# Normed rows on ScalarE, their scale and sum on GpSimd, and a later place for the second norm's means, in a fused tokenizer, scan and experts kernel

## The chip, the cores and the metric

The kernel runs on one core of one Trainium2 chip. The metric is the device time of one launch in microseconds (us), as the median of several runs. A core has five engines that work side by side: TensorE (PE in the rows; its weight loads are PEld), VectorE (DVE), ScalarE (ACT), GpSimd (POOL) and SyncE (SP), which here only issues DMAs. Each takes its instructions in the order written for it, and stands still where one of them waits for a semaphore. [...]

## The reference

Images become tokens, a selective scan mixes them, and a mixture of experts follows. What the change touches is the layer norm before the scan, the layer norm after it, the residual sum, and the statistics of the third norm. Cut down:

```
h = concat(tokens(x), txt)                      # 4 x 384 rows of 192 channels
a = in_proj(layernorm(h))                       # first norm
u = silu(conv(a_x)); dt = softplus(u @ dt_w.T + dt_b)
s_t = exp(dt * A_n) * s_(t-1) + dt * B_n * u    # for each of 16 states n
y = sum_n(C_n * s_n) + D * u
r = (y * silu(a_z)) @ out_w.T + layernorm(h)
h = h + (r - mean(r)) / std(r) * ln_g + ln_b    # second norm, scale, shift
logits = layernorm(h) @ Wr.T                    # third norm; top 2 of 8 experts
h = h + experts(layernorm(h))
```

## The kernel before

The 1536 rows are held as 12 tiles of 128 rows, in NJ = 3 groups j of NB = 4 tiles; `h_tok[:, j, b, :]` is one tile with its 192 channels. A group is also a chunk of 128 time steps. The scan goes through 48 steps: `at` runs from 0 to 47, the chunk is n = at // 16 and the state is s = at % 16. Chunk 0 still has the first norm, projections and convolution of the last group mixed into it; chunks 1 and 2 have the output of the chunk before mixed in.

One step `at` is spread over all engines, and each engine's order is written out by hand:

- SP issues the broadcast of row C of the step (`broadcast_c`, three DMAs, as soon as the product three steps back is done), sometimes a row B (`broadcast_b`), and a part of the experts' weights (`load_expert`). At steps 30 and 46 it also waits for `xf_rdy` and sends a group's router rows to DRAM (`send_rows`).
- TensorE spreads row B over the partitions (`spread_b(at)`, L983 to L986, except for steps with at % 6 == 5), does the step's extra work or a filler (L1053), and then adds the product of two steps back into `sums` (`sum_states(at - 2)`, L1005 and L1007). So `spread_b(at)` stands behind `sum_states(at - 3)` in its queue.
- ScalarE saves the last state of the chunk (`save_carry`, L1443), brings the state carried over from the chunk before (`bring_carry(at + 1)`, L1455; it waits for `spread_b(at + 1)`), and makes exp(dt * A) (`decay_of(at + 2)`, L1437 and L1438). At step 24 (and 40) follow `deviation` (Sqrt, L1306) for the second norm, at 25 (41) for the third norm, and at 28 (44) `router_rows` (L1462), which makes the third norm's rows. Changing between Exp and Sqrt costs a table load.
- VectorE multiplies by row B (L1752, not in the steps with at % 6 == 5) and runs the scan over all six blocks of channels (L1760). In front of scan 24 `residual` takes means and variances of the output rows in PSUM (`means`, L1586 and L1591) and makes (r - mean) * ln_g (`normed_rows`, L1776). Behind scan 24 come the reciprocal (`inverse`, L1602), four small operations on the router's scores, `new_h` (L1807, h + that * rstd) with the third norm's means, and behind scan 26 `row_shift` (L1602, L1816). Steps 39 to 42 repeat it for group 1. After the last step group 2 is done in pieces.
- GpSimd multiplies the states by row C (L697, product `at`; waits for scan `at`), and for the steps with at % 6 == 5 also by row B (`pool_drive`, L686). At step 24 (40) it first waits for `h_new`, and at 26 (42) for `shift_rdy`, so that these products don't start earlier. `add_shift` (L661) adds ln_b to a group of h.

Two buffers hold the states, so scan `at` waits for product `at - 2` and for the carry of step `at - 2`. The rows of the first norm of the last group are made by VectorE behind scan 4 (`input_norm(2)`, L1606); TensorE's transposes, and GpSimd's product 4, wait for them (`xn_ready`).

```
elif s == 8:                       # GpSimd, before
    pool.wait_ge(h_new, n)
elif s == 10:
    pool.wait_ge(shift_rdy, n)
```

Of the kernel before, what the change touches and what calls it, by code (L numbers as in the profile page):

```python
# [19 lines left out]
ALU = mybir.AluOpType  # L20
# [3 lines left out]
P = 128  # L24
NB = 4
C = 192
CB = C - P
NJ = 3
# [115 lines left out]
def build(nc, d, out):  # L144
    with ExitStack() as ctx:
# [26 lines left out]
        shift = sb("shift", [P, NT])  # L172
        bo = sb("bo", [P, C])
# [227 lines left out]
        shift_rdy = sem("shift_rdy")  # L401
        top_step = sem("top_step")
# [123 lines left out]
        def _(sp):  # L526
# [77 lines left out]
            for at in range(RING, STEPS):  # L604
                if at == S - 3:
                    store_bc(2)
                broadcast_c(at)
                if at == S - 2:
                    sp.wait_ge(bc_stored, 16 * 8)
                if by_pool(at - RING) and at - RING + 6 < STEPS:  # L610
                    broadcast_b(at - RING + 6)
                if at > S and at % S == 14:
                    send_rows(at // S - 1)
                if at == S:
                    sp.wait_ge(xt_ready, 6)
                    sp.wait_ge(dtu_rdy, 3)
                if at == 2 * S + 7:
                    sp.wait_ge(summed, 2 * S + 1)
                    sp.dma_start(u_cm[:, 0:N_TAB // 2], d["cst"][:, N_CST:N_CST + N_TAB // 2]).then_inc(ld_tab, 16)
                if at >= S and at % 4 != 3 and loaded < len(loads):  # L620
                    load_expert(*loads[loaded], PIECES)
                    loaded += 1
            assert loaded == len(loads)
            sp.wait_ge(summed, STEPS)
            for e in range(E - LATE, E - 1):
                load_expert(e, 0, 1)
            send_rows(2)
# [15 lines left out]
        def _(pool):  # L643
# [19 lines left out]

            def inserted_work(n, s):

                if n == 0:
                    if s == 4:
                        pool.wait_ge(xn_ready, 3)
                    elif s == 7:
                        pool.wait_ge(conv_step, 8 * 3)  # L670
                    elif s == 11:
                        pool.wait_ge(split_step, 5 * 3)
                    elif s == 13:
                        pool.wait_ge(dtu_rdy, 3)
                elif s == 8:
                    pool.wait_ge(h_new, n)
                elif s == 10:
                    pool.wait_ge(shift_rdy, n)
# [10 lines left out]
            for at in range(STEPS - 1):  # L689
                if at in (1, 5, S + 2):  # L690
                    add_shift(at // 4 if at < S else 2)
                pool.wait_ge(scanned, at + 1)
# [517 lines left out]
        def _(act):  # L1210
# [206 lines left out]

            act.wait_ge(a_exp, 2)
# [51 lines left out]
            for at in range(STEPS):  # L1470
# [9 lines left out]
                if n == 0:  # L1480
# [4 lines left out]
                    elif s == 4:  # L1485
                        deviation(2)
                    elif s == 5:
# [24 lines left out]
                else:  # L1512
                    if s == 8:
                        deviation(1 + 2 * n)
                    elif s == 9:
                        deviation(2 + 2 * n)
                    elif s == 12:
                        router_rows(n - 1)
# [37 lines left out]
        def _(dve):  # L1556
# [95 lines left out]

            def input_norm(n):
                j = JS[n]
                inverse()
                for b in range(NB):
# [122 lines left out]
            def residual(j):  # L1779
                dve.wait_ge(attn_ps, j + 1)  # L1780
                means([attn_rows(j, b)[:, 0:C] for b in range(NB)])
                for b in range(NB):
                    ins = normed_rows(j, b)
                ins.then_inc(rr_rdy, 1)
                dve.wait_ge(rr_rdy, j + 1)
# [18 lines left out]
            def new_h(j):  # L1804
# [4 lines left out]
                ins.then_inc(h_new, 1)  # L1809
                dve.wait_ge(h_new, j + 1)  # L1810
# [28 lines left out]
            for at in range(STEPS):  # L1839
# [14 lines left out]
                else:  # L1854
# [4 lines left out]
                    elif s == 8:  # L1859
                        if n == 1:  # L1860
                            dve.wait_ge(hb_rdy, NJ)
# [3 lines left out]
                        new_h(n - 1)  # L1865
# [3 lines left out]
                    elif s == 10:  # L1869
# [61 lines left out]
            dve.wait_ge(rr_rdy, NJ + 1)  # L1931
            new_h(2)
# [171 lines left out]
```

## Time and profile before

| | us |
|---|---|
| median of 3 runs | 431.66 |
| lowest, highest | 430.48, 434.25 |
| span of the profiled execution | 431.6 |

| scan step (L1760) | starts at | | scan step | starts at |
|---|---|---|---|---|
| 4 | 90.52 | | 30 | 183.36 |
| 7 | 99.08 | | 33 | 191.79 |
| 16 | 137.79 | | 35 | 197.02 |
| 23 | 155.69 | | 36 | 202.01 |
| 24 | 161.39 | | 39 | 210.18 |
| 25 | 169.23 | | 40 | 215.88 |
| 26 | 172.85 | | 41 | 221.69 |
| 28 | 178.48 | | 46 | 236.28 |
| 29 | 180.34 | | 47 | 238.02 |

The profile's times count from the first instruction. The span agrees with the median to 0.1 us, so sums made inside the profiled execution can be read against the median directly. The scan is the stretch from 78 to 240 us; before it lie the first two norms and projections, behind it the routing (to 269) and the experts (to the end). The rows show for each instruction its start, its length, its engine, line and tiles, and in brackets how long the engine stood idle in front of it and who released it.

### The profile page before, as it was taken

To read this page: it belongs to the slowest core of one execution; us is meant where nothing else is said; L and a number is where in the kernel's file an instruction comes from. 1 tells how busy PE (TensorE), PEld (TensorE's weight loads), DVE (VectorE), ACT (ScalarE), POOL (GpSimd) and SP (SyncE) were. 2 spreads that over 40 slices of the span, in tenths; PEclk is the share of its full clock that TensorE was granted. 3 is DMA by queue.
4 is the path that set the end of the run, shared out by engine and by line. 5 is a ranking of instruction groups with operands and counts; after the bars stand their busy time and mean duration, and the time that the engine had idled before them with its cause. 6 is when DMAs were issued, how large, how long until landed. Compare 5 with 4: busy or idle time off the path is not lost.

```text
span 431.6 us, 6906 instructions
## 1 busy us (share of the span) xinstructions
PE 379.8 (88%) x2285; PEld 286.8 (66%) x2285; DVE 276.2 (64%) x511; ACT 200.5 (46%) x516; POOL 224.0 (52%) x166
## 2 busy tenths in 40 slices
PE   5799989979996995779968898999999999999970
PEld 4465756646564662445634486799999999999970
DVE  4605456999899998997999596643444534434400
ACT  1347447674853546734547023144444354354440
POOL 6877730564636772756637200345565554655531
PEclk9969899999989996998979997799999999999995
DMA  6401103446574875497857544433333233232224
GB/s 168 78 6 11 7 3 70 122 120 137 116 147 122 232 243 165 158 270 210 294 167 189 150 209 74 113 83 59 49 46 61 43 49 56 44 52 48 39 28 118
DMA packets 37351, 46.98 MB, mean 109 GB/s; under 512 B 9485, under 2 KB 25950, under 8 KB 36750
## 3 DMA queue, kind: packets, MB, share of 16 engines
q1 hardware_dynamic: 29998, 38.94, 32.1%
q0 software_dynamic: 7328, 7.74, 12.2%
q8 instruction: 12, 0.20, 0.2%
q14 instruction: 13, 0.11, 0.1%
HBM read 40.65 MB, written 7.19 MB: 111 GB/s over the span
## 4 chain that ended last, share of the span: by engine, by line
PE 60%; DVE 17%; ACT 6%; DMA 5%; POOL 5%; issue 3%; SPq 1%; POOLq 0%; DVEq 0%; ACTq 0%
PE ps L1190 15%; PE ps L1171 10%; PE ps L1179 6%; DVE w_all L1760 5%; PE ps L1005 4%; DMA w_all<-bc_dram 3%; PE ps L1053 3%; PE ps L934 3%; POOL w_all L647 3%; POOL w_all L697 2%; DVE ps L1752 2%; PE ps L1007 2%; PE ps L1161 2%; DVE stats L1586 1%; DVE h_tok L1807 1%
## 5 line engine op out<-in xcount | busy, mean ns | idle before, releaser
L697 POOL TENSOR_TENSOR w_all<-w_all 128x768 f32<-128x768 f32 x47 | 78.9, 1682 | 82.4 <-DVE w_all L1760 36.6
L722 POOL DMA_INDIRECT sum_dram<-u_cm,tok_row x31 | 50.9, 1641 | 60.5 <-ACT u_cm L1551 53.8
L1005 PE MATMUL ps<-w_all,cst 128*128 128x512 f32 x96 | 55.4, 661 | 22.9 <-POOL w_all L697 22.3
L1760 DVE TENSOR_TENSOR_SCAN w_all<-decay,ps 128x780 f32<-128x780 f32 x40 | 71.1, 1779 | 2.0 <-POOL w_all L697 0.7
L706 POOL DMA_INDIRECT dt_cm<-x_dram,tok_in x31 | 30.8, 993 | 41.0 <-DVE texi L1989 29.0
L647 POOL DMA_INDIRECT w_all<-in_pix,gidx x42 | 44.1, 1051 | 14.9 <-issue 12.5
L1536 ACT ACTIVATE u_cm<-ps,x_cm 128x128 f32<-128x128 f32 x96 | 26.5, 376 | 39.8 <-PE ps L1179 39.8
L934 PE MATMUL ps<-cst 128*128 128x256 f32 x132 | 36.5, 433 | 5.5 <-DMA cst<-in_cst 4.9
L1005 PEld LDWEIGHTS ps<-w_all,cst 128*128 128x128 f32 x96 | 16.5, 198 | 35.4 <-POOL w_all L697 30.4
L1752 DVE TENSOR_TENSOR ps<-dtu_cm,ps 128x768 f32<-128x768 f32 x40 | 38.0, 949 | 2.7 <-ACT ps L1455 2.5
L1536 ACT ACTIVATE z_cm<-ps,y_cm 128x128 f32<-128x128 f32 x90 | 24.8, 375 | 27.5 <-PE ps L1179 27.5
L934 PEld LDWEIGHTS ps<-cst 128*128 128x128 f32 x132 | 28.0, 219 | 12.6 <-DMA cst<-in_cst 4.9
L2001 DVE COPY x_cm<-w_all 128x1154 f32 x16 | 12.2, 762 | 37.1 <-PE ps L1190 37.1
L1007 PEld LDWEIGHTS ps<-w_all,cst 128*128 128x128 f32 x96 | 19.2, 200 | 24.9 <-issue 24.9
L1190 PE MATMUL ps<-x_cm,u_cm 128*128 128x192 f32 x192 | 35.5, 333 | 0.0
L1053 PE MATMUL ps<-cst 128*128 128x256 f32 x122 | 33.6, 401 | 0.0
L1190 PE MATMUL ps<-y_cm,z_cm 128*128 128x192 f32 x180 | 33.4, 334 | 0.0
L2001 DVE COPY y_cm<-w_all 128x1154 f32 x15 | 11.4, 762 | 33.0 <-PE ps L1190 33.0
L1437 ACT ACTIVATE decay<-dt_cm,a_neg 128x512 f32<-128x512 f32 x40 | 28.4, 711 | 8.2 <-DVE dt_cm L1709 8.1
L1190 PEld LDWEIGHTS ps<-x_cm,u_cm 128*128 128x128 f32 x192 | 31.0, 189 | 1.8
L1190 PEld LDWEIGHTS ps<-y_cm,z_cm 128*128 128x128 f32 x180 | 29.0, 189 | 1.8
L1007 PE MATMUL ps<-w_all,cst 128*128 128x256 f32 x96 | 30.1, 396 | 0.0
(268 smaller groups left out, 706.8 us busy)
## 6 DMA issues: line engine op xcount, KB each, us to landing
w_all<-bc_dram SPq DMA_DIRECT2D x48, 256.0 KB, 3.6
w_all<-bc_dram SPq DMA_DIRECT2D x96, 64.0 KB, 3.8
w_all<-in_w_all SPq DMA_DIRECT2D x20, 289.0 KB, 4.5
w_all<-in_w_all SPq DMA_DIRECT2D x3, 1156.0 KB, 8.9
b_wide_sb<-bc_dram SPq DMA_DIRECT2D x8, 256.0 KB, 3.9
x_dram<-x_cm SPq DMA_DIRECT2D x3, 384.0 KB, 4.6
sum_dram<-h_tok SPq DMA_DIRECT2D x3, 384.0 KB, 4.3
out<-sum_dram SPq DMA_DIRECT2D x4, 288.0 KB, 3.7
```

What stands on the lines that cost most here:

```text
L647: pool.indirect_dma_start(dst, None, d[table], bass.IndirectOffsetOnAxis(ap=gidx[:, col:col + 1].bitcast(U32), axis=0)).then_inc(signal, 16)
L697: nc.gpsimd.tensor_tensor(segments(hcs[at % 2]), inner(states[at % 2]), segments(c_sb[at % RING]), ALU.mult).then_inc(hc_rdy, 1)
L722: pool.indirect_dma_start(sum_dram, bass.IndirectOffsetOnAxis(ap=tok_row[:, i:i + 1].bitcast(U32), axis=0), y_out[:, i % 2, :], None, comp ...
L934: nc.tensor.matmul(ps[:, bank, 0:256], ident, cst[:, 0:256], start=True, stop=True)
L1005: nc.tensor.matmul(sums[:, 0:4 * P], ident, hcs[at % 2][:, 0:4 * P], start=False, stop=at % S == S - 1, skip_group_check=True)
L1007: nc.tensor.matmul(sums[:, 4 * P:6 * P], ident, hcs[at % 2][:, 4 * P:6 * P], start=False, stop=at % S == S - 1, skip_group_check=True).the ...
L1053: nc.tensor.matmul(ps[:, bank, 256:512], ident, cst[:, 0:256], start=False, stop=True, skip_group_check=True)
L1171: nc.tensor.matmul(ps[:, 2 + 2 * p + f // 3, P * (f % 3):P * (f % 3) + P], w[:, W_UA + P * f:W_UA + P * f + P], xe[:, p, 0:P], start=(f % ...
L1190: mm = nc.tensor.matmul(ps[:, 6 + p, 0:C], hid[p][:, P * f:P * f + P], w_now[p][:, W_DN + C * f:W_DN + C * f + C], start=(f == 0), stop=(f ...
L1536: ins = nc.scalar.activation(hid[p][:, P * f:P * f + P], ps[:, 2 + 2 * p + f // 3, P * (f % 3):P * (f % 3) + P], ACT.Gelu, bias=w_now[p][: ...
L1752: v.tensor_tensor(inner(wide(p)), chunk(dtu3, n), inner(wide(p)), ALU.mult).then_inc(driven, 1)
L1760: v.tensor_tensor_scan(states[p], fade, drive, 0.0, ALU.mult, ALU.add).then_inc(scanned, 1)
```

## The change

For groups 0 and 1 (chunks 1 and 2) the second norm's rows move from VectorE to ScalarE, as Identity with scale rstd and bias -mean * rstd (`fall`, one small VectorE operation, `row_fall`). GpSimd multiplies them by ln_g in two operations of 128x384 at s == 9 (`scale_rows`) and adds them to h in two more at s == 11 (`add_rows`), which now signals `h_new`. VectorE takes the third norm's means at s == 12 and the row shift at s == 13; ScalarE takes that norm's deviation at s == 13 and the router rows at s == 14. GpSimd's two waits at s == 8 and s == 10 go. The first norm of the last group is made by ScalarE too. SP sends group 0's rows at step 34 instead of 30, and group 1's behind the last step instead of at 46. Group 2's norm after the scan stays on VectorE.

```diff
@@ sync
-                if at > S and at % S == 14:
-                    send_rows(at // S - 1)
+                if at == 2 * S + 2:
+                    send_rows(0)
...
                 load_expert(e, 0, 1)
+            send_rows(1)
             send_rows(2)
@@ gpsimd
+            def scale_rows(j):
+                pool.wait_ge(rows_normed, j + 1)
+                for two in (ip_a, ip_b):
+                    rows = two[:, :].rearrange("p (b c) -> p b c", b=2)
+                    ins = nc.gpsimd.tensor_tensor(rows, rows, ln_gb[:, 0:1, :].to_broadcast([P, 2, C]), ALU.mult)
+                ins.then_inc(scaled, 1)
+
+            def add_rows(j):
+                pool.wait_ge(scaled, j + 1)
+                for h, two in ((0, ip_a), (1, ip_b)):
+                    ins = nc.gpsimd.tensor_tensor(h_tok[:, j, 2 * h:2 * h + 2, :], h_tok[:, j, 2 * h:2 * h + 2, :],
+                                                  two[:, :].rearrange("p (b c) -> p b c", b=2), ALU.add)
+                ins.then_inc(h_new, 1)
...
-                elif s == 8:
-                    pool.wait_ge(h_new, n)
-                elif s == 10:
-                    pool.wait_ge(shift_rdy, n)
...
+                if at >= S and at % S == 9:
+                    scale_rows(at // S - 1)
+                elif at >= S and at % S == 11:
+                    pool.wait_ge(hb_rdy, NJ)
+                    add_rows(at // S - 1)
                 pool.wait_ge(scanned, at + 1)
@@ scalar
+            def last_input_rows():
+                j = JS[2]
+                act.wait_ge(fall_rdy, 1)
+                for b in range(NB):
+                    t = NB * j + b
+                    ins = nc.scalar.activation(xn[:, j, b, 0:C], h_tok[:, j, b, :], ACT.Identity, bias=fall[:, 0, t:t + 1],
+                                               scale=rstd[:, 0, t:t + 1])
+                ins.then_inc(xn_ready, 1)
+
+            def normed_rows(j):
+                act.wait_ge(fall_rdy, j + 2)
+                if j:
+                    act.wait_ge(h_new, j)
+                for b in range(NB):
+                    t = NB * j + b
+                    ins = nc.scalar.activation(rr(b), attn_rows(j, b)[:, 0:C], ACT.Identity, bias=fall[:, 1, t:t + 1],
+                                               scale=rstd[:, 1, t:t + 1])
+                ins.then_inc(rows_normed, 1)
...
                     elif s == 4:
                         deviation(2)
+                        last_input_rows()
...
                     if s == 8:
                         deviation(1 + 2 * n)
-                    elif s == 9:
+                        normed_rows(n - 1)
+                    elif s == 13:
                         deviation(2 + 2 * n)
-                    elif s == 12:
+                    elif s == 14:
                         router_rows(n - 1)
@@ vector
+            def row_fall(norm, j):
...
+                v.scalar_tensor_tensor(fall[:, norm, t], mv[:, norm, t, 0], -1.0, rstd[:, norm, t], ALU.mult, ALU.mult)\
+                    .then_inc(fall_rdy, 1)
...
                 inverse()
+                if n == 2:
+                    row_fall(0, j)
+                    return
...
                 means([attn_rows(j, b)[:, 0:C] for b in range(NB)])
-                for b in range(NB):
-                    ins = normed_rows(j, b)
-                ins.then_inc(rr_rdy, 1)
-                dve.wait_ge(rr_rdy, j + 1)
...
                     elif s == 8:
-                        if n == 1:
-                            dve.wait_ge(hb_rdy, NJ)
                         inverse()
                         unscaled_scores(n - 1)
                         router_scores(n - 1)
-                        new_h(n - 1)
+                        row_fall(1, n - 1)
                     elif s == 9:
                         largest(n - 1)
                         its_experts(n - 1)
-                    elif s == 10:
+                    elif s == 12:
+                        h_means(n - 1)
+                    elif s == 13:
                         row_shift(n - 1)
```

`h_means` is the second half of `new_h` (wait for `h_new`, then the means of the group of h). `new_h` itself is left for group 2 alone, under the name `last_h`, and waits there for `hb_rdy`.

## Rows read from the trace of the kernel before

**Rows 1.** The cores: span and mean granted clock
```profile
core 0: 431.6 us, clock 0.941
```

**Rows 2.** Stretches from:to, length, busy us (count) by engine, clock, DMA share, GB/s
```profile
158.00:184.00 26.00, 18.23 (x72) 10.47 (x71) 24.09 (x54) 17.03 (x40) 13.39 (x8) 0.87 0.56 175
```

**Rows 3.** Who waited for whom, 130 to 245 us: total us, times, longest us
```profile
POOL w_all L697 <- DVE h_tok L1807: 11.9, 2, 7.2
```

**Rows 4.** Timeline, VectorE, chunk 0 (start, length, operation, [idle before])
```profile
92.40 1.25 DVE L1606 TENSOR_SCALAR xn<-h_tok,mv,rstd 128x192 f32<-128x192 f32 x4
99.08 1.78 DVE L1760 TENSOR_TENSOR_SCAN w_all<-decay,ps 128x780 f32<-128x780 f32 x1 [0.21 <-POOL w_all L697]
```

**Rows 5.** Timeline, GpSimd: product 4
```profile
93.78 1.68 POOL L697 TENSOR_TENSOR w_all<-w_all 128x768 f32<-128x768 f32 x1 [3.24 <-DVE xn L1606]
```

**Rows 6.** Timeline, VectorE, step 24 to scan 26
```profile
158.97 0.74 DVE L1776 SCALAR_TENSOR_TENSOR ip_a<-ps,mv,ln_gb 128x192 f32<-128x192 f32 x2
...
164.09 0.18 DVE L1602 RECIPROCAL rstd<-std 128x4 f32<-128x4 f32 x1 [0.93 <-ACT std L1306]
...
165.21 0.75 DVE L1807 SCALAR_TENSOR_TENSOR h_tok<-ip_a,rstd,h_tok 128x192 f32<-128x192 f32 x2
...
166.65 1.14 DVE L1586 BATCH_NORM_STATS2 stats<-h_tok 128x6 f32<-128x192 f32 x4
...
169.23 1.78 DVE L1760 TENSOR_TENSOR_SCAN w_all<-decay,ps 128x780 f32<-128x780 f32 x1
...
172.85 1.78 DVE L1760 TENSOR_TENSOR_SCAN w_all<-decay,ps 128x780 f32<-128x780 f32 x1
...
174.73 0.16 DVE L1816 SCALAR_TENSOR_TENSOR shift<-mv,rstd 128x4 f32<-128x4 f32 x1
```

**Rows 7.** Timeline, ScalarE, steps 24 to 30
```profile
163.90 0.20 ACT L1443 ACTIVATE carry<-w_all 128x6 f32<-128x6 f32 x1
...
172.14 0.18 ACT L1455 ACTIVATE ps<-carry 128x6 f32<-128x6 f32 x1 [0.88 <-PE ps L986]
172.34 1.28 ACT L1437 ACT_TABLE_LOAD   x1
173.63 0.72 ACT L1437 ACTIVATE decay<-dt_cm,a_neg 128x512 f32<-128x512 f32 x1
174.26 0.49 ACT L1438 ACTIVATE decay<-dt_cm,a_neg 128x256 f32<-128x256 f32 x1
...
179.91 1.85 ACT L1462 ACTIVATE x_cm<-h_tok,shift,rstd 128x192 f32<-128x192 f32 x4
...
182.15 0.18 ACT L1455 ACTIVATE ps<-carry 128x6 f32<-128x6 f32 x1 [0.29 <-PE ps L986]
```

**Rows 8.** Timeline, TensorE: sums of product 24, of 27, and of 40
```profile
168.47 2.07 PE L1005 MATMUL ps<-w_all,cst 128*128 128x512 f32 x2 [4.31 <-POOL w_all L697]
...
180.17 1.12 PE L1005 MATMUL ps<-w_all,cst 128*128 128x512 f32 x2 [1.42 <-POOL w_all L697]
...
221.94 2.08 PE L1005 MATMUL ps<-w_all,cst 128*128 128x512 f32 x2 [3.28 <-POOL w_all L697]
```

**Rows 9.** The page's groups by line, and by form: GpSimd (busy us, mean ns, idle before)
```profile
L697 POOL TENSOR_TENSOR w_all<-w_all 128x768 f32<-128x768 f32 x47 | 78.9, 1682 | 82.4 <-DVE w_all L1760 36.6 <-DVE h_tok L1807 11.9 <-DVE dtu_cm L1711 8.0
L686 POOL TENSOR_TENSOR decay<-dtu_cm,b_wide_sb 128x768 f32<-128x768 f32 x8 | 14.5, 1817 | 0.0
L661 POOL TENSOR_TENSOR h_tok<-h_tok,ln_gb 128x768 f32<-128x768 f32 x3 | 5.5, 1817 | 0.0
L2094 POOL MEMSET const-uint8-127<- 128x1 uint8 x1 | 0.1, 119 | 0.0
```

**Rows 10.** Timeline, VectorE, chunk 2: what it waited for
```profile
201.01 0.96 DVE L1752 TENSOR_TENSOR ps<-dtu_cm,ps 128x768 f32<-128x768 f32 x1 [2.24 <-ACT ps L1455]
...
240.90 0.96 DVE L1836 TENSOR_TENSOR w_all<-w_all 128x768 f32<-128x768 f32 x1 [1.09 <-DMA w_all<-bc_dram]
243.50 0.96 DVE L1764 TENSOR_TENSOR y_cm<-ps,z_cm 128x768 f32<-128x768 f32 x1 [1.65 <-PE ps L1007]
```

More of the change, by code:

```diff
@@ L172, in build @@
         shift = sb("shift", [P, NT])
+        fall = sb("fall", [P, 2, NT])
         bo = sb("bo", [P, C])
@@ L401, in build @@
         shift_rdy = sem("shift_rdy")
+        fall_rdy = sem("fall_rdy")
+        rows_normed = sem("rows_normed")
+        scaled = sem("scaled")
         top_step = sem("top_step")
@@ L1651, in input_means @@
                 means([h_tok[:, JS[n], b, :] for b in range(NB)])
+            falls = 0
+            def row_fall(norm, j):
+                nonlocal falls
+                falls += 1
+                t = slice(NB * j, NB * j + NB)
+                v.scalar_tensor_tensor(fall[:, norm, t], mv[:, norm, t, 0], -1.0, rstd[:, norm, t], ALU.mult, ALU.mult)\
+                    .then_inc(fall_rdy, 1)
             def input_norm(n):
@@ L1802, in router_scores, with last_h @@
                 scored(v.tensor_tensor(logit[:, t, :], logit[:, t, :], p1[:, t, :], ALU.add))
-            def new_h(j):
+            def last_h():
+                j = NJ - 1
                 for b in range(NB):
@@ L1809, in new_h, with h_means @@
                 ins.then_inc(h_new, 1)
+                h_means(j)
+            def h_means(j):
                 dve.wait_ge(h_new, j + 1)
@@ L1930, in _ @@
             ins.then_inc(rr_rdy, 1)
-            dve.wait_ge(rr_rdy, NJ + 1)
-            new_h(2)
+            dve.wait_ge(rr_rdy, 2)
+            dve.wait_ge(hb_rdy, NJ)
+            last_h()
             rt(v.tensor_tensor(gtmp[:, 1, :], top_v[:, :, 1], top_v[:, :, 0], ALU.subtract))
```

## The prediction, made before the changed kernel ran

> **What bounds the kernel now.** I read the cores first: the span is 431.6 us [rows 1], equal to the median. The change lies in the scan, so I went by stretches: while group 0's output is mixed in, VectorE is busy 24.1 of 26 us [rows 2]. Then the timelines. The scan goes at VectorE's pace, some 2.7 us a step (0.96 and 1.78, less their overlap [rows 10]), except where a wait shows: 0.93 for the standard deviation behind scan 24 [rows 6]; 2.24 at step 36 and 1.09 for the last row C [rows 10]. GpSimd waits much longer for h_new, 11.9 us in two places [rows 3], but its product is wanted only two scans later. So taking work from VectorE is worth its time where VectorE has the last word, and nothing where ScalarE, TensorE or GpSimd have it. The question is which of them is late next.
>
> **What is removed.** VectorE loses four L1776 and four L1807 in each of two groups. A pair takes 0.74 [rows 6], four of a kind 1.4, so 2.8 a group; and L1606 with 1.25 [rows 4]. It gains three `row_fall` like L1816 with 0.16 [rows 6]. Net 2 x 2.8 + 1.25 - 0.5 = 6.4 us less. The third norm's means are moved, not removed: 1.14 [rows 6] and 0.38 for the four aggregates, 1.5.
>
> **Prices of what is added.** ScalarE: four Identity rows of 192 with scale and bias take 1.85 [rows 7]. GpSimd: no 128x384 operation is in the trace. The 128x768 ones take 1.68 to 1.82, the smallest memset 0.12 [rows 9], so little of the price is fixed and a half costs 0.85 to 0.95; two make 1.85. The other bound is that a half costs as much as a whole, 1.8 each.
>
> [...]
>
> Whether Identity wants a table of its own behind Sqrt no row shows; a load is 1.28 [rows 7], and the nearest row is a Copy straight behind the Sqrt, without one [rows 7]. I take nothing, and keep 1.28 for the range.
>
> [...]
>
> **Chunk 0, +0.85.** VectorE ended the input rows at 92.40 + 1.25 = 93.65 [rows 4], and product 4 followed at once [rows 5]. Now: `row_fall` to 92.6, ScalarE's four to 94.5. VectorE is free 1.1 earlier and scan 5 moves up, but product 4 starts 0.85 later, behind it GpSimd's `add_shift` and product 5, and scan 7 already waited 0.21 for that product [rows 4]. TensorE's projection also follows the same rows. Both paths move by 0.85, and nothing up to chunk 1 takes it back. Below I use the old clock, without this shift.
>
> **Chunk 1, to step 30.**
> - Without L1776 scan 24 starts 1.4 earlier. But the standard deviation comes at 164.0 as before: ScalarE reaches it behind its carry and decay, which hang on TensorE's queue. The wait of 0.93 becomes 2.3. Gain nothing.
> - Behind the reciprocal the scores end at 165.21 [rows 6]. L1807 and the means go from there (1.4 + 1.5, to 168.2), `row_fall` comes. Scan 25 starts at 166.35 instead of 169.23, 2.9 ahead; scan 26 at 166.35 + 3.62 (the old distance [rows 6]) = 169.97, to 171.75.
> - ScalarE's rows take 165.4 to 167.3, GpSimd's scale to 169.2, product 25 to 170.9. Scan 27 wants it at 172.65 or later: hidden.
> - GpSimd then has product 26 (from 171.85), the row-B product for step 29, `add_rows`, product 27: 1.65 + 1.77 + 1.85 + 1.65 = 6.9, to 178.75. That is the new late one. The means of step 28 start at 177.1 (`h_new`) and end at 178.7, and scan 29 waits for product 27: 178.8 to 180.6, 1.45 ahead.
> - TensorE adds product 27 and only then spreads row B of step 30; ScalarE's carry for 30 waits for that, then comes decay 31, and *then* the moved `deviation`. This is the worst place of the change. Old distance from the sum's start to ScalarE's carry: 180.17 to 182.15 = 2.0 at full clock, 168.47 to 172.14 = 3.7 where TensorE had idled 4.31 [rows 7, 8]. TensorE idles here from about 175.5 to 178.8, 3.3 us. Idles of 3.28 and 4.31 were followed by a sum at half pace (2.08 and 2.07), one of 1.42 was not [rows 8]; I take the slow one. The carry ends at 180.9 or 182.6.
> - Decay 0.72 + 0.49 less overlap 1.1, load 1.28 [rows 7], and 0.3 for the Sqrt (the four-element operations beside it take 0.2): 2.7. The deviation is there at 183.6 or 185.3, where VectorE has been idle since 180.6. With `row_shift` 0.35 and the row-B product 0.95 scan 30 starts at 185.0 or 186.7, before 183.36: 1.6 or 3.3 behind, after having been 3.1 ahead at scan 28.
>
> **Chunk 1, to step 36.** ScalarE's load, decay, router rows (4.2 together) and carry end about 1 us before scan 31 does: hidden, barely. `send_rows(0)` no longer holds up SP at step 30, so the rows C of steps 31 and 32 come in time, TensorE isn't starved at 189 to 192, and most of the 2.24 at step 36 [rows 10] and another 0.4 in front of step 33 go. At step 34 the same 384 KB lie before row C of step 35, which has over 2 us to spare. Step 36 is 0.35 ahead (full clock) or 1.2 behind (slow): I take 1.05 behind.
>
> **Chunk 2, -2.2.** Here VectorE waited for no deviation, so the first 1.4 count too: 1.4 + 2.9 = 4.3 ahead at scan 41 and 4.4 at 44. Step 44 gives back 1.5 for the means: 2.8 ahead. There is no row-B product of GpSimd between product 42 and `add_rows(1)`, so product 43 is in time and the deviation comes at 232.2, just before scan 45 ends; at the slow clock 1.1 late. Decay 47 stands behind a table load, about 0.4. The 1.09 for the last row C goes, since SP has no `send_rows` in front of it, but the sums of 46 and 47 must still follow each other on TensorE. `chunk_output(2)` was at 243.50 [rows 10]; it comes at 240.7 (2.8 ahead) or 241.75 (1.75 ahead). Middle 2.2. Behind it nothing changes; `send_rows(1)` has 20 us to land.
>
> **Sum.** 431.6 + 0.85 + 1.05 - 2.2 = 431.3 us. The saving of 6.4 and the two waits are nearly all spent on ScalarE's and GpSimd's later answers.
>
> **Rivals.**
> 1. *The same path, TensorE at full clock.* 431.6 + 0.85 - 0.35 - 2.8 = 429.3. For it: busy work is pulled forward, the old idle of 4.31 goes. Against: the new idle of 3.3.
> 2. *VectorE has the last word throughout* (faster). All 6.4 count, and the 2.24: 431.6 - 8.6 = 423.0. For it: it is busy 93% of this stretch [rows 2]. Against: the order on ScalarE at step 29, and the two waits already there. It needs the deviation of step 29 ready by 181.
> 3. *GpSimd's halves cost as much as wholes* (slower). Scale and sum take 3.6 each: product 25 ends at 172.7 and pushes product 26 by 0.85, the sum pushes product 27 by another 1.8, so 2.65 in chunk 1, and some 3 in chunk 2 by the same queue. 431.3 + 5.7 = 437.0. Against: the memset's 0.12 [rows 9]. It passes 1% from about 1.6 us for a half.
> 4. *Identity loads a table*: 1.28 at each of three places on the path, 431.3 + 3.8 = 435.1, within 1%.
>
> **How the numbers follow.** One per cent, 4.3 us, is about what a measurement of this kernel can tell from no change. Forecast 0.46, rival 1 0.22, rival 2 0.14, rival 3 0.10, rival 4 0.04; 0.04 for other losses over 1%. So faster 0.14, same 0.72, slower 0.14. The time is that of the likeliest, 431.3. The range leaves out rivals 2 and 3 with most of their chance, and takes in 1 and 4 with 1.3 us below 429.3 for links that I have sized by one row: 428.0 to 435.1.
>
> **What would show it.** Scan 7 at about 99.9. Scan 25 2.9 nearer to scan 24's old place. The four ScalarE rows 1.85, GpSimd's halves 0.85 to 0.95. VectorE idle about 3 to 4.5 us in front of the reciprocal between scans 29 and 30, released by ScalarE; TensorE idle over 3 us before the sum of product 27, and the granted clock at 0.5 behind it. No DMA wait before the last product, and none of 2 us before step 36. If the reciprocal in front of step 30 waits for nothing, rival 2 is right; if the halves take over 1.6, rival 3.

## The result, and the profile after

The changed kernel takes 434.69 us (median of 20 runs, 430.16 to 439.77); the kernel before takes 432.45 us in the same comparison (20 runs, 428.08 to 440.05). The ratio is 1.0059, with a 95% interval of 1.0034 to 1.0084: about 2.5 us slower, 1.5 to 3.6. I had forecast 431.3 us and no change. The time lies in my range, the sign doesn't agree.

The page of the kernel after (busy us, share of the span, instructions). Before, VectorE was busy for 276.2 us, ScalarE for 200.5 and GpSimd for 224.0:

```profile
PE 377.9 (88%) x2285; PEld 285.8 (67%) x2285; DVE 272.5 (63%) x494; ACT 205.7 (48%) x528; POOL 229.9 (53%) x174
```

```profile
core 0: 429.8 us, clock 0.948
```

The clock is the one granted to TensorE on the mean, as a share of full speed.

VectorE did get 3.7 us less work (I had reckoned with 6.4; 1.5 of the difference is the row shift of 1.67 us shown below, which counts as busy time), and the span is even 1.8 us shorter than that of [rows 1]. Neither is the result. The spans differ in their long tail and in the time up to scan 4, which the change doesn't touch: scan 4 starts at 85.4 to 93.5 us from one execution to another, of either order. So I compare the stretches between starts of scans. "End" is the last `chunk_output(2)` (L1764, now L1822). Each number is worked out from the timeline of VectorE:

| scans | before | before, 2nd | after | after, 2nd |
|---|---|---|---|---|
| 4 to 16 | 47.27 | 47.28 | 49.41 | 47.72 |
| 16 to 28 | 40.69 | 40.67 | 37.83 | 37.85 |
| 28 to 30 | 4.88 | 4.89 | 9.22 | 9.22 |
| 30 to 36 | 18.65 | 16.48 | 16.47 | 16.46 |
| 36 to 40 | 13.87 | 13.87 | 12.44 | 12.45 |
| 40 to 44 | 15.06 | 15.06 | 13.11 | 11.92 |
| 44 to 47 | 7.08 | 7.09 | 10.41 | 10.40 |
| 47 to end | 5.48 | 5.06 | 4.77 | 4.78 |
| sum | 152.98 | 150.40 | 153.66 | 150.80 |

Most stretches repeat to 0.02 us. The others belong to an execution: the 2.2 us that I read in the kernel before (30 to 36) isn't in its second execution, and the kernel after has two of that kind (4 to 16, 40 to 44).

What is given back between scans 28 and 30: the timelines of VectorE and ScalarE of the kernel after (start, length, operation, idle before).

```profile
176.14 1.78 DVE L1818 TENSOR_TENSOR_SCAN w_all<-ps,decay 128x780 f32<-128x780 f32 x1
180.81 0.18 DVE L1647 RECIPROCAL rstd<-std 128x4 f32<-128x4 f32 x1 [2.89 <-ACT std L1328]
```

```profile
177.95 0.18 ACT L1498 ACTIVATE ps<-carry 128x6 f32<-128x6 f32 x1 [3.05 <-PE ps L1008]
178.06 0.71 ACT L1480 ACTIVATE decay<-dt_cm,a_neg 128x512 f32<-128x512 f32 x1
178.68 0.49 ACT L1481 ACTIVATE decay<-dt_cm,a_neg 128x256 f32<-128x256 f32 x1
179.18 1.28 ACT L1328 ACT_TABLE_LOAD   x1
180.48 0.30 ACT L1328 ACTIVATE std<-mv,cst 128x4 f32<-128x4 f32 x1
```

VectorE stands 2.89 us for a Sqrt of 0.30, behind a carry, a decay and a table load. What is given back in chunk 2, VectorE and GpSimd:

```profile
219.81 0.96 DVE L1810 TENSOR_TENSOR ps<-dtu_cm,ps 128x768 f32<-128x768 f32 x1 [0.45 <-ACT ps L1498]
...
223.12 0.96 DVE L1810 TENSOR_TENSOR ps<-dtu_cm,ps 128x768 f32<-128x768 f32 x1 [0.53 <-ACT ps L1498]
...
230.25 1.67 DVE L1874 SCALAR_TENSOR_TENSOR shift<-mv,rstd 128x4 f32<-128x4 f32 x1
```

```profile
215.20 1.68 POOL L719 TENSOR_TENSOR w_all<-w_all 128x768 f32<-128x768 f32 x1 [2.56 <-DMA w_all<-bc_dram]
...
230.22 1.68 POOL L719 TENSOR_TENSOR w_all<-w_all 128x768 f32<-128x768 f32 x1 [0.81 <-DVE w_all L1818]
```

The row shift over 128x4 took 0.16 us in [rows 6] and takes 1.67 here. It starts 0.03 us behind product 45 of GpSimd and ends with it. The profile shows no idle time for it: the loss is inside an instruction's length.

### The profile page after: what moved, and what is told of

Same layout as the page of the kernel before. It is cut to its first block, busy times and chain, and to the rows that moved or that the text cites. A ratio compares the mean times of both kernels' runs of the same rounds, so it can differ in the third digit from the quotient of the medians.

```text
span 429.8 us, 6909 instructions
## 1 busy us (share of the span) xinstructions
PE 377.9 (88%) x2285; PEld 285.8 (67%) x2285; DVE 272.5 (63%) x494; ACT 205.7 (48%) x528; POOL 229.9 (53%) x174
## 3 DMA queue, kind: packets, MB, share of 16 engines
q0 software_dynamic: 7328, 7.74, 12.3%
## 4 chain that ended last, share of the span: by engine, by line
PE 59%; DVE 15%; ACT 7%; POOL 7%; DMA 4%; issue 4%; SPq 1%; POOLq 0%; DVEq 0%; ACTq 0%
PE ps L1212 15%; PE ps L1193 10%; PE ps L1201 6%; DVE w_all L1818 5%; PE ps L1027 4%; POOL w_all L719 3%; DVE ps L1810 2%; POOL w_all L652 2%; PE ps L956 2%; DMA w_all<-bc_dram 2%; PE ps L1075 2%; PE ps L1029 2%; PE ps L1183 2%; ACT decay L1480 1%; PE ps L890 1%
## 5 line engine op out<-in xcount | busy, mean ns | idle before, releaser
L744 POOL DMA_INDIRECT sum_dram<-u_cm,tok_row x31 | 49.7, 1602 | 63.2 <-ACT u_cm L1596 60.6
L956 PE MATMUL ps<-cst 128*128 128x256 f32 x132 | 35.8, 426 | 5.5 <-DMA cst<-in_cst 4.9
L1075 PE MATMUL ps<-cst 128*128 128x256 f32 x122 | 33.0, 395 | 0.0
```

Source lines behind the costliest of these rows:

```text
L744: pool.indirect_dma_start(sum_dram, bass.IndirectOffsetOnAxis(ap=tok_row[:, i:i + 1].bitcast(U32), axis=0), y_out[:, i % 2, :], None, comp ...
L956: nc.tensor.matmul(ps[:, bank, 0:256], ident, cst[:, 0:256], start=True, stop=True)
L1075: nc.tensor.matmul(ps[:, bank, 256:512], ident, cst[:, 0:256], start=False, stop=True, skip_group_check=True)
```

## The experiments

Sums below are scan 4 to the end, as in the table. A ratio is against the kernel before on the same chip.

**The kernel before, and the kernel after, once more** (nothing is edited; one execution each).

> The kernel before once more, for a second profile. Theory 5: the 2.2 us stall in front of step 36, which I counted as removed, belongs to some executions only (e2, which keeps the transfer at step 30, doesn't have it): scan 30 to 36 takes 16.5 us here. Rival: the stall belongs to the kernel and takes 18.6 again; then e2's 16.5 comes from its shift of 0.8 us.

> A further execution of the changed kernel itself. The stretches that the instructions' order sets should repeat within 0.1 us: 28 to 30 9.2, 44 to 47 10.4, 24 to 28 15.7, 36 to 40 12.4. Where TensorE's clock chooses, it may differ: 4 to 7 10.2 if the loss of chunk 0 belongs to the kernel, 9.4 if it belongs to the execution shown first.

They are the columns "2nd" above. The stall of step 36 is in some executions of the kernel before only. Of the loss in chunk 0, 1.7 of 2.1 us, and 1.2 us of chunk 2 belong to the first execution of the kernel after. The two least disturbed executions differ by 0.4 us only (150.80 against 150.40).

TensorE, product 31's sum and the fillers behind it, in the kernel before, first the execution of [rows 10]:

```profile
191.65 1.13 PE L1005 MATMUL ps<-w_all,cst 128*128 128x512 f32 x2 [2.37 <-POOL w_all L697]
...
193.74 2.77 PE L1053 MATMUL ps<-cst 128*128 128x256 f32 x6
```

and its second execution:

```profile
189.69 1.13 PE L1005 MATMUL ps<-w_all,cst 128*128 128x512 f32 x2 [1.89 <-POOL w_all L697]
...
191.42 1.46 PE L1053 MATMUL ps<-cst 128*128 128x256 f32 x6
```

GpSimd waits 3.01 and 2.54 us for row C there. In the first TensorE idled 2.37 us and the six fillers took 2.77 us instead of 1.46. Windows over this place (length, busy time of PE, PEld, DVE, ACT, POOL, then granted clock, DMA share, GB/s), the first from the kernel before, the second from its second execution:

```profile
190.00:196.20 6.20, 4.55 (x14) 3.37 (x15) 5.71 (x6) 2.31 (x8) 6.20 (x4) 0.74 0.94 288
```

```profile
188.00:192.70 4.70, 3.01 (x14) 2.16 (x15) 4.67 (x5) 1.71 (x6) 4.70 (x3) 1.00 0.91 297
```

**The last input rows back on VectorE, and on ScalarE alone.**

```diff
@@ the changed kernel, rows on VectorE again
-                if n == 2:
-                    row_fall(0, j)
-                    return
...
-                        last_input_rows()
@@ the kernel before, rows on ScalarE
+                        last_input_rows()
...
+                if n == 2:
+                    t = slice(NB * j, NB * j + NB)
+                    v.scalar_tensor_tensor(fall[:, 0, t], mv[:, 0, t, 0], -1.0, rstd[:, 0, t], ALU.mult, ALU.mult)\
+                        .then_inc(fall_rdy, 1)
+                    return
```

> The changed kernel, with the last group's input rows back on VectorE (its L1606), all else kept. [...] Theory 2 (the wait of 2.9 us for the deviation behind scan 29) and theory 3 (the moved row transfers make the end later): it stays at 1.005, with at most 0.9 us gained.

> The kernel before, with only the last group's input rows moved to ScalarE. [...] Theories 2 and 3: slower by the 0.85 us that I forecast, 1.002, the clock unchanged.

Back on VectorE: ratio 1.0014 (0.9959 to 1.0070), chunk 0 as before, 47.29. On ScalarE alone: ratio 1.0008 (0.9961 to 1.0056), 0.8 us more between scans 4 and 7 and 0.35 less between 8 and 16, so 47.73. Moving these rows costs 0.4 us where TensorE keeps its clock. It did in six of the seven executions with the rows on ScalarE: from 2.5 to 8 us behind the start of ScalarE's rows the granted clock was 1.00 in the six and 0.69 in the seventh. So the whole loss of 0.6% doesn't lie in chunk 0: ScalarE's rows alone cost 0.4 us and not the 2.1 of the first execution of the kernel after, and the profile with the rows back on VectorE has a sum of 153.97, no less than the 153.66 of the kernel after. In the seventh execution, the kernel after as shown first, the clock fell. Windows from scan 5 on, kernel after and its second execution:

```profile
90.30:100.00 9.70, 9.14 (x47) 5.27 (x48) 6.14 (x7) 5.95 (x15) 6.14 (x4) 0.82 0.45 115
```

```profile
95.40:105.00 9.60, 9.03 (x56) 5.70 (x56) 7.53 (x10) 6.76 (x16) 6.15 (x4) 1.00 0.45 117
```

TensorE had idled 1.24 and 1.66 us just before in both.

**Fillers in front of the transposes of these rows.**

```diff
                     elif s == 6:
+                        filler(4)
                         norm_transposes(2)
```

> The changed kernel with four fillers of TensorE in front of the transposes of the last input rows (step 6), which TensorE ran behind an idle of 1.66 us in all executions with the rows on ScalarE, while its clock fell behind them in one of four. The theory that this idle decides expects it cut to about 1 us or less and, from scan 4 to 7, 9.4 us as at full clock. The rival, that the clock at this place hangs on what came earlier, allows 10.2 here too. One execution can refute the first and only lean towards it.

9.36 from scan 4 to 7, with a granted clock of 1.00 from 94.80 to 100.30 (sum 151.27, one run of 433.65). The unedited kernel has 9.36 too in its second execution, so this run tells nothing about the idle. It is inconclusive.

**The second deviation in front of the carry and the decay.**

```diff
@@ scalar, step s == 13
+                    deviation(2 + 2 * n)
                     bring_carry(at + 1)
                     decay_of(at + 2)
...
-                    elif s == 13:
-                        deviation(2 + 2 * n)
```

> The changed kernel, with ScalarE's third-norm deviation of step 29 (and 45) put in front of the carry and decay of that step instead of behind them. Theory 2: VectorE's wait of 2.9 us in front of the reciprocal goes, the Exp table's load then lies in front of decay 31, hidden beside scans 29 and 30; 2.5 us faster than the changed kernel, 1.000 of before. [...]

The stretch from 28 to 30 takes 7.74 us instead of 9.22, a gain of 1.5 us where I expected 2.5, and the ratio is 1.0076 (1.0037 to 1.0115), no better. The reciprocal no longer waits, but the row shift behind it runs beside product 29. VectorE and GpSimd of this run:

```profile
184.03 0.15 DVE L1647 RECIPROCAL rstd<-std 128x4 f32<-128x4 f32 x1
184.21 1.67 DVE L1874 SCALAR_TENSOR_TENSOR shift<-mv,rstd 128x4 f32<-128x4 f32 x1
```

```profile
184.19 1.67 POOL L719 TENSOR_TENSOR w_all<-w_all 128x768 f32<-128x768 f32 x1 [0.45 <-DVE w_all L1818]
```

**Only SP's transfers moved** (twice).

```diff
@@ the kernel before, sync
-                if at > S and at % S == 14:
-                    send_rows(at // S - 1)
+                if at == 2 * S + 2:
+                    send_rows(0)
...
+            send_rows(1)
             send_rows(2)
```

> The kernel before, with only SP's two row transfers moved (group 0 to step 34, group 1 behind the last step). By my sum: the stall of 2.2 us at step 36, 0.4 in front of scan 33 and part of the 1.1 for the last row C go: 2 to 3.5 us faster, 0.992 to 0.995. Theory 3: the transfer behind the experts' weights or the one at step 34 costs as much at the end or later: 1.000 to 1.005.

> The kernel before with only the moved transfers of the router rows, once more: it tells whether the moved transfers are worth something by themselves. If the stall of 2.24 us at step 36 in the profile of before is in some of its executions only, and the wait for the last row C (1.1 us) in all, the transfers are worth about 0.4 (47 to the last output, 5.06 to 4.74) plus a share of 2.2: a ratio of 0.995 to 0.999. If the stall were in all executions, 0.993 or below. If the transfers do nothing, 1.000. From scan 30 to 36 16.5 us.

Ratios 0.9941 (0.9894 to 0.9987) and 0.9970 (0.9935 to 1.0004); sums 150.07 and 150.05, without the stall, and 4.74 us from scan 47 to the end. This is the part of the change that is worth something by itself, 0.3 to 0.6 per cent; the second interval just includes no change. With the transfer at step 30 the stretch from 30 to 36 took 18.65, 16.48, 16.46, 16.87 and 18.75 us in five executions; without it never more than 16.86 in fourteen.

**GpSimd's two waits taken from the kernel before, and one given to the changed kernel.**

```diff
@@ the kernel before, gpsimd
-                elif s == 8:
-                    pool.wait_ge(h_new, n)
-                elif s == 10:
-                    pool.wait_ge(shift_rdy, n)
@@ the changed kernel, gpsimd
+                elif s == 13:
+                    pool.wait_ge(shift_rdy, n)
```

> The kernel before, without GpSimd's two waits (for h_new at steps 24 and 40, for shift_rdy at 26 and 42), nothing else changed; its products read and write none of those tensors. Theory 4 (a VectorE operation with two SBUF inputs stands still while a GpSimd product runs, as the 1.67 us row shift of the changed kernel at step 45 and of e3 at step 29 suggest): row_shift in steps 26 and 42 takes 1.67 instead of 0.16, some L1807 of group 1 take up to 1 us more; from scan 24 to 28 it is 1.5 us longer (18.6), from 40 to 44 1.5 to 2.3 longer (16.6 to 17.3), in all 3 to 4 us slower, 1.007 to 1.009. Rival: the 1.67 is a wait of another kind (a late semaphore), then both stretches keep 17.1 and 15.1 and the time is that of before or less.

> The changed kernel, with a wait of GpSimd for shift_rdy put in front of product 29 and 45. Theory 4: the row shift of step 45 takes 0.16 again, scan 44 to 47 takes 8.9 us instead of 10.4, and the kernel is 1.5 us faster than the changed one, 1.002 of before. Rival: no change in that stretch.

Without the waits the kernel before loses 2.0 us from 24 to 28 and 2.8 us from 40 to 44; its ratio is 1.0102 (1.0039 to 1.0166). Its row shift takes 1.67:

```profile
177.37 1.67 DVE L1812 SCALAR_TENSOR_TENSOR shift<-mv,rstd 128x4 f32<-128x4 f32 x1
```

```profile
177.34 1.68 POOL L693 TENSOR_TENSOR w_all<-w_all 128x768 f32<-128x768 f32 x1 [1.93 <-DVE w_all L1756]
```

That is 1.5 us in each chunk. The rest is the same clash at other operations. In chunk 1 the first operation of the scores starts 1.06 us behind product 24, takes 0.66 us instead of 0.19 and ends with the product (0.5 us). In chunk 2 the first two L1803 (L1807 in the kernel before) start 0.18 us behind product 40 and take 2.05 us instead of 0.74 (1.3 us):

```profile
166.47 0.66 DVE L1789 TENSOR_TENSOR logit<-mv,g_sum 128x32 f32<-128x32 f32 x1
...
220.91 2.05 DVE L1803 SCALAR_TENSOR_TENSOR h_tok<-ip_a,rstd,h_tok 128x192 f32<-128x192 f32 x2
```

```profile
165.41 1.68 POOL L693 TENSOR_TENSOR w_all<-w_all 128x768 f32<-128x768 f32 x1 [3.65 <-DMA w_all<-bc_dram]
...
220.73 1.68 POOL L693 TENSOR_TENSOR w_all<-w_all 128x768 f32<-128x768 f32 x1 [2.81 <-DMA w_all<-bc_dram]
```

VectorE's multiplication by row B, with one input in PSUM, keeps its 0.94 us although it starts in the middle of product 25:

```profile
174.51 0.94 DVE L1748 TENSOR_TENSOR ps<-dtu_cm,ps 128x768 f32<-128x768 f32 x1
```

```profile
173.73 1.68 POOL L693 TENSOR_TENSOR w_all<-w_all 128x768 f32<-128x768 f32 x1 [6.64 <-DVE w_all L1756]
```

With one wait the changed kernel gains what was expected, 8.90 instead of 10.41 from 44 to 47, and its ratio is 0.9970 (0.9920 to 1.0020). VectorE and GpSimd of that run, the same place as the 1.67 of the kernel after:

```profile
232.83 0.16 DVE L1876 SCALAR_TENSOR_TENSOR shift<-mv,rstd 128x4 f32<-128x4 f32 x1
```

```profile
233.13 1.68 POOL L721 TENSOR_TENSOR w_all<-w_all 128x768 f32<-128x768 f32 x1 [1.13 <-DVE shift L1876]
```

Product 45 starts 0.4 us behind its scan instead of 0.1, and nobody misses it. The sum of product 45 on TensorE, in the second execution of the kernel after and in this run:

```profile
238.66 1.12 PE L1027 MATMUL ps<-w_all,cst 128*128 128x512 f32 x2 [2.90 <-POOL w_all L719]
```

```profile
237.50 1.12 PE L1029 MATMUL ps<-w_all,cst 128*128 128x512 f32 x2 [1.07 <-POOL w_all L721]
```

The clash also opens an idle of 2.90 us on TensorE. In six executions without the wait (the idle was 2.90 us in five and 2.29 in one) a sum behind the idle ran slowly in three (1.92 to 2.08 us instead of 1.02 to 1.12), and scan 47 to the end took 6.2 to 6.5 us instead of 4.8; in the six executions with the wait it was 4.8 or 4.9 each time.

**All three mends** (input rows on VectorE, deviation first, GpSimd's wait), twice.

> The changed kernel with the three mends together: last group's input rows on VectorE, deviation in front of carry and decay, GpSimd's wait for shift_rdy at steps 29 and 45. If the parts add: chunk 0 as before (8.6 and 7.3 us), scan 28 to 30 6.2 us instead of 9.2, scan 44 to 47 8.9 instead of 10.4. From scan 16 to 47 2.9 us less than before without its stall at step 36; with the moved transfers 0.987 to 0.991 of before. If another wait takes their place: 0.995 or more.

> The kernel with all three mends once more, for an interval: the changed kernel, with the last input rows back on VectorE, the second deviation of a chunk in front of the carry and the decay, and GpSimd waiting for the row shift. Its profile had 4.0 us less than an undisturbed execution of the kernel before from scan 4 to the chunk's last output (146.4 against 150.4). The theory that VectorE's work does count once the late answers and the clash with GpSimd are gone expects a ratio of 0.991 (4.0 of 432), 0.985 to 0.996. The rival, that the low median of the earlier runs came from where TensorE's clock happened to stand in them, expects 0.998 to 1.002. From scan 28 to 30 6.3 us and from 44 to 47 8.9 us in both.

The first comparison gives 428.19 us (6 runs, before 433.26; no ratio), the second 427.81 with a ratio of 0.9869 (0.9832 to 0.9906): 5.7 us faster than the kernel before. From 28 to 30 it is 6.28 and 6.29 us, from 44 to 47 8.91. The sums are 146.40 and 149.01; they differ in the stretch from 40 to 44, with 11.98 and 14.46. With the moved transfers alone the sums were 150.07 and 150.05.

**The transfer of 1 MB behind the row.** In the second profile of the three mends product 40 waited 4.28 us for row C, and SP issues 1 MB (`u_cm<-in_cst`, for the routing) at step 39, in front of that row.

```profile
211.58 1.69 POOL L721 TENSOR_TENSOR w_all<-w_all 128x768 f32<-128x768 f32 x1 [4.28 <-DMA w_all<-bc_dram]
```

```diff
-                if at == 2 * S + 7:
+                if at == 2 * S + 11:
```

> The changed kernel with SP's transfer of 1 MB (the routing table, into u_cm) issued at step 43 instead of step 39, where it lies in front of row C of step 40. If the row's lateness is what varied, scan 40 to 44 takes 11.9 us (four steps of 2.67 and 1.26 of small operations) and product 40 waits 0.5 us at most; from 44 to 47 10.4 as before. In time 0.9 us less than the changed kernel's mean, a ratio of 1.000 to 1.005 against the kernel before. If something else makes it vary, 40 to 44 stays between 12 and 14. What could spoil it: the 1 MB now lies in front of rows C of 46 and 47 and a wait shows before the last product.

> The three mends (last input rows on VectorE, second deviation in front of carry and decay, GpSimd waiting for the row shift) and the transfer of 1 MB at step 43. Its last execution took 14.46 us from scan 40 to 44, with product 40 4.28 us late. The theory expects 11.9 here, and a ratio of 0.982 to 0.987 against the kernel before (0.987 without the move, of which up to 0.006 can come back). The rival expects 0.987 as before.

> The kernel before with the transfer of 1 MB at step 43, as a control. Its product 40 waits for h_new, 6 us and more behind its row C, so the theory expects 15.06 us from scan 40 to 44 and a ratio of 0.998 to 1.003. If the transfer held up more than that one row, a gain shows here too, as 0.995 or less.

Product 40 no longer waits for a DMA, and the stretch gets longer: 14.66 and 14.80 us. The ratios are 1.0136 (1.0049 to 1.0222), 0.9951 (0.9893 to 1.0009) and, for the kernel before, 0.9997 (0.9953 to 1.0042), whose 15.06 stays. My theory was half right: the row's lateness had gone, but it had done a service. VectorE and GpSimd behind scan 40, changed kernel with the transfer moved:

```profile
212.99 0.15 DVE L1647 RECIPROCAL rstd<-std 128x4 f32<-128x4 f32 x1
213.17 1.70 DVE L1847 TENSOR_TENSOR logit<-mv,g_sum 128x32 f32<-128x32 f32 x1
214.90 0.19 DVE L1850 TENSOR_TENSOR logit<-ps,logit 128x32 f32<-128x32 f32 x1
```

```profile
213.15 1.68 POOL L719 TENSOR_TENSOR w_all<-w_all 128x768 f32<-128x768 f32 x1 [1.10 <-DVE w_all L1818]
```

The first operation of the scores stands beside the early product, 1.70 us for 0.19. The next one starts when the product has ended and costs 0.19 again. That is 1.5 of the 2.7 us. The rest comes at step 43. GpSimd's product 41 is late, TensorE idles 2.68 us before its sum, the sum takes 2.08 us instead of 1.12, and VectorE waits for the carry behind it. Both executions with the transfer moved have this idle and this slow sum. TensorE and VectorE of the first:

```profile
221.21 2.08 PE L1027 MATMUL ps<-w_all,cst 128*128 128x512 f32 x2 [2.68 <-POOL w_all L719]
```

```profile
224.95 0.96 DVE L1810 TENSOR_TENSOR ps<-dtu_cm,ps 128x768 f32<-128x768 f32 x1 [1.12 <-ACT ps L1498]
```

**GpSimd waits for these small operations too,** in chunk 2, with the transfer at step 43 and at step 39.

```diff
+                elif s == 8 and n == 2:
+                    pool.wait_ge(fall_rdy, n)
```

> The three mends, the 1 MB transfer at step 43, and in chunk 2 GpSimd waits for VectorE's small operations (fall_rdy) before product 40, which now starts 1.3 us behind scan 40. If the clash with the first operation of the scores (1.70 for 0.19) is what lengthened the stretch, it takes 0.19 again and scan 40 to 44 11.9 to 12.0 us, 2.8 less than with the transfer moved alone, in every execution; the ratio against the kernel before is 0.982 to 0.988. If product 40's lateness of 1.3 us costs something itself (as 2.56 did: 1.2), 12.0 to 12.5. If the rest of the stretch was slowed by something else, 14 again.

> The same with the 1 MB transfer at step 39, as in the changed kernel. Where row C of step 40 comes late the wait for the small operations changes nothing: 11.9 to 14.5 us from scan 40 to 44 by how late it is, a ratio of 0.984 to 0.991. If the transfer doesn't matter once the clash is excluded, 11.9 as in the other.

12.01 and 12.32 us, the 0.19 is back, and the sums are 146.41 and 146.74. The first is at 424.9 us against 432.98 (ratio 0.9859, 0.9797 to 0.9922), the second at 428.34 (0.9880, 0.9820 to 0.9941). By the intervals I can't rank them, nor set them apart from the three mends.

How much later product 40 starts than scan 40 ends, and what the stretch from 40 to 44 takes, in twelve executions:

| product 40 behind scan 40 | first score operation | 40 to 44 |
|---|---|---|
| 0.07, 0.08 | 1.70 | 14.80, 14.66 |
| 1.07, 1.30 | 0.19 | 11.92, 12.01 |
| 1.57, 1.72, 1.73, 1.78 | 0.19 | 12.32, 12.27, 11.98, 12.36 |
| 2.42, 2.52 | 0.19 | 13.11, 12.79 |
| 2.89, 3.58 | 0.19 | 13.82, 14.46 |

The lateness doesn't set the length alone: TensorE's granted clock from scan 40 to 44 differs between these executions too (0.78 to 1.00), and the sum of product 41 took 1.02 to 2.08 us in them.

## Why the prediction was wrong, point by point

My forecast by chunk against the executions, in us (positive is longer; scan 4 to 16, 16 to 36, 36 to the end). The last column takes the mean of the executions in which the stretch has the order of the kernel after (seven, five, five) less the mean of those that have the order of the kernel before:

| | forecast | after less before, as profiled | the second executions | mean |
|---|---|---|---|---|
| chunk 0 | +0.85 | +2.14 | +0.44 | +0.7 |
| chunk 1 | +1.05 | -0.70 | +1.49 | +0.4 |
| chunk 2 | -2.2 | -0.76 | -1.53 | -0.2 |
| sum | -0.3 | +0.68 | +0.40 | +0.8 |

Chunk 1 looks better than forecast only where a disturbed execution of the kernel before is in the comparison. Chunk 2 gives less than forecast in every column.

**Right: where VectorE waits.** The reciprocal at step 24 waited 2.28 us (forecast 2.3), and removing L1776 gained nothing there. Scan 28 came 2.86 us ahead (forecast 3.1). ScalarE's four rows took 1.86 us for the input rows and 1.71 or 1.72 for a group of the second norm (two of 0.91 in a row, overlapping), and the Identity loaded no table (the rows at 162.57 stand behind the Sqrt at 160.92 with no load between them); scan 41 came 4.3 us ahead in the second execution. A half on GpSimd took 0.99 to 1.02, above my 0.85 to 0.95, four halves being some 0.4 us more; no rival about its price was needed. For one operation of 128x768 without PSUM, [rows 9] and [rows 10] have 1.68 us on GpSimd (L697) and 0.96 on VectorE (L1836), a factor of 1.75. The reciprocal at step 29 stood 2.89 us, released by ScalarE, as the worst place of the change.

**Right in place, not in clock: step 30.** From 16 to 30 the kernel after takes 47.05 us against 45.57: 1.5 behind, where I had 1.6 at full clock and took 3.3. I expected an idle of over 3 us of TensorE before the sum of product 27 and a slow sum. The rows of after, first the earlier sum of product 25, are these:

```profile
168.00 2.08 PE L1027 MATMUL ps<-w_all,cst 128*128 128x512 f32 x2 [1.78 <-POOL w_all L719]
...
175.96 1.12 PE L1027 MATMUL ps<-w_all,cst 128*128 128x512 f32 x2 [1.16 <-POOL w_all L719]
```

TensorE had run slowly from 168.00 on (granted clock 0.60 from 168 to 175, 1.00 from 174.8 to 180) and was thereby busy until 174.8. So rival 1 was right about this stretch.

**Wrong, the step "Chunk 1, to step 36": a stall of one execution counted as removed.** I took the 2.24 us of [rows 10] and another 0.4 as a property of the kernel before. They are in 2 of 5 executions of its order with the transfer at step 30, so a gain of 2.2 us is worth 0.9 on the mean. The step counts on 2 us gained between scans 30 and 36. Against the profile itself it held, 30 to 36 did lose 2.18; between the second executions it is 0.02 (16.48 and 16.46). The 1.05 that I entered for this chunk lies near the slow end of its two values (0.35 ahead, 1.2 behind) without a working. Against the median of many runs it was 1.3 us too good. Linked to it, I took the profiled execution for the median because 431.6 equalled 431.66; but a span lies 1.8 us below its run's time (429.8 and 431.58), so that execution was slower than the median.

**Wrong, the missing step: GpSimd's waits priced at nothing.** I listed the removal of the two waits and costed it nowhere. Two effects came of it, both in chunk 2, where VectorE waits for no deviation.
- *Too early.* The row shift of step 45 ran beside product 45: 1.5 us, and TensorE's idle of 2.90 us behind it, with another 1.6 us in three of six executions. This is the largest part of what "Chunk 2, -2.2" lacks, and the wait put back returned just it (10.41 to 8.90): with it the chunk took 38.40 us, 2.7 less than in the second execution of before. In chunk 1 the same clash was hidden only because ScalarE's deviation was later still; it appeared as soon as that was mended.
- *Too late.* Before, product 40 waited for `h_new`, for 4.77 us in the profile of before, and a late row C was hidden behind that. Now its lateness reaches VectorE: 40 to 44 took 11.92 to 14.46 us in eight executions, 12.84 on the mean, where I had 12.06 (15.06, and from 1.4 ahead to 4.4). Up to 2.5 us above the shortest, 0.9 on the mean.

With both, the chunk from scan 36 on took 40.73 and 39.55 us in the two executions of the kernel after, and 43.14, 41.83 and 39.98 in three kernels that run it alike: 41.05 on the mean. The order of before took 41.49, 41.08, 41.14 and 41.39. So on the mean 0.2 us are gained where I had 2.2.

**Chunk 0, +0.85: mis-sized.** The loss is 0.4 us at a granted clock of 1.00, since 0.35 comes back behind scan 8, where I wrote that nothing takes it back. In one execution of seven the clock fell there (0.82 from 90.30 to 100.00) and the loss was 2.1 us.

**Where the 2.5 us are.** Least disturbed against least disturbed the changed kernel is 0.4 us longer. On the mean of the profiled executions add 0.9 for the late row, 0.2 for chunk 0's clock, and take off the 0.9 of the old stall for the kernel before: that makes 0.6, and 0.8 for the last stretch, 1.6 us longer in three of six. This is reckoned and not measured, and reaches 1.4 of a measured 1.5 to 3.6; the means by chunk in the table above reach only 0.8. The rest, 1.1 to 1.7 of the 2.5 us, stays open. A few profiles can't settle it, as the parts outside the change vary by 8 us between them. Shown is that the wait put back brings the kernel to 0.9970 (0.9920 to 1.0020), and all three mends to 0.9869.

**The clash that I left out.** In each of these cases a VectorE operation with two SBUF inputs that started within a product of GpSimd ended with it, to 0.04 us: 0.16 became 1.67 and 0.19 became 1.70 when started 0.02 to 0.03 us behind a product of 1.68, 0.19 became 0.66 when started 1.06 behind it, and the multiplication with an input in PSUM kept its 0.94. That speaks against removing GpSimd's waits. With the 1.5 us (1.68 less 0.16, both in the rows of before) of one such clash my sum would have been 432.8 us, an estimate, and a reason to doubt the plan without `shift_rdy`.

## What to carry to other kernels

A wait that looks like pure loss (11.9 us of GpSimd in [rows 3]) can be what keeps a long product off a neighbour's small operations on the critical path (the row shift took 1.67 us beside it and 0.16 without). Before you remove one, ask what will then run side by side, and what lateness it used to hide. Before you count a stall as removed, look for it in a second execution of the same kernel. Moving work off the busiest engine and the row transfers together paid here, 1.3% in all (the transfers alone gave 0.3 to 0.6), but only once the answers it waits for were put in front of carry and decay and GpSimd was held back for 0.3 to 1.3 us at two or three places.

## What the runs showed of the hardware that I had not expected

- A VectorE operation over 128x4 with both inputs in SBUF took 1.67 us beside GpSimd's product of 1.68, and 0.16 without. The profile books it as busy time, so no list of waits shows it. Look for a mean that changes.
- The same order of instructions with the same idles of TensorE (1.24 and 1.66 us) was followed by a granted clock of 0.82 in one execution and of 1.00 in five (and in the one with fillers between). In the kernel before it stayed at 1.00 after an idle of 1.89 us and was 0.74 after 2.37. But after 2.90 the next sums kept their 1.1 us in three of five executions. What happens at a given gap is not a property of the kernel alone.
- Taking away the lateness of a row's DMA made the kernel slower in that stretch (11.92 to 14.46 us in eight executions with the DMA late, 14.66 and 14.80 without), since the lateness had kept the product out of the way of VectorE's small operations. With the product held back by a semaphore instead it took 12.01.
